# A graph layer on one core: the first layer norm folded into centred weights, with its row factors sent through DRAM

## The reference, cut to what matters

```
def _layernorm(x, axis=-1, eps=1e-05):
    m = jnp.mean(x, axis=axis, keepdims=True)
    v = jnp.var(x, axis=axis, keepdims=True)
    return (x - m) / jnp.sqrt(v + eps)

# graph layer: N_USER = N_ITEM = 10000, HID = 128
h = item_feat @ W_item.T + b_item
b = user_feat @ W_user.T + b_user
gnn = jax.nn.relu(adj @ h + b)

# an LSTM over the 10000 rows, then gated running sums of its states
x = x + gnn(_layernorm(x), ...)           # adj is 10000 x 10000, float32
x = x + ffn(_layernorm(x)[None], ...)[0]
```

## Time and profile before

| | us |
|---|---|
| median of 3 runs (1485.9 to 1490.18) | 1486.9 |
| the profiled execution | 1486.99 |
| its span, first to last instruction | 1485.2 |

### The profile page before, as it was taken

One profiled execution on the slowest core, in us unless ns is written; L12 is line 12 of the kernel. 1 busy time (PEld: TensorE's weight loads), 2 busy tenths in 40 slices (PEclk: granted clock), 3 DMA queues, 4 the chain that ended last, 5 costly groups with the idle time before them and its releaser, 6 DMA issues.

```text
span 1485.2 us, 25012 instructions
## 1 busy us (share of the span) xinstructions
PE 1449.2 (98%) x7584; PEld 1227.4 (83%) x7584; DVE 1218.3 (82%) x2027; ACT 1088.3 (73%) x1601; POOL 212.8 (14%) x189
## 2 busy tenths in 40 slices
PE   8999999999999999999999999999999799999994
PEld 7878888788778888888888888877888699999994
DVE  7998888888888888888888888888888566677677
ACT  5778777778777778777777787777778476556662
POOL 0000010000001001001001000000100032017775
PEclk9999999999999999999999999999999899999997
DMA  9889999999999999999999999999999203000003
GB/s 382 309 325 359 376 345 360 367 350 365 358 352 361 370 351 363 371 356 358 367 352 371 352 359 376 340 369 355 350 363 380 97 1 123 15 2 0 0 0 139
DMA packets 70515, 426.67 MB, mean 287 GB/s; under 512 B 8723, under 2 KB 17620, under 8 KB 70358
## 3 DMA queue, kind: packets, MB, share of 16 engines
q1 hardware_dynamic: 68896, 425.12, 76.6%
q10 hardware_dynamic: 1590, 1.18, 0.2%
HBM read 416.02 MB, written 10.24 MB: 287 GB/s over the span
## 4 chain that ended last, share of the span: by engine, by line
issue 79%; PE 19%; DVE 1%; POOL 0%; ACT 0%; POOLq 0%; DVEq 0%
PE psZ L848 10%; PE psZ L836 3%; PE psZ L837 2%; PE psZ L838 2%; PE psZ L854 1%; DVE u L1241 1%; PE psZ L824 0%; PE psZ L914 0%; POOL rstd L419 0%; POOLq L422 0%; ACT normed L557 0%; PE psZ L918 0%; DVE dif L1256 0%; PE psV L734 0%; DVE dif L1254 0%
## 5 line engine op out<-in xcount | busy, mean ns | idle before, releaser
L998 DVE TENSOR_TENSOR a_lo<-raw,a_hi 128x1000 fp32r<-128x1000 f32 (+1 forms) x800 | 917.3, 1182 | 108.4 <-ACT a_hi L586 101.9
L586 ACT ACTIVATE a_hi<-raw 128x1000 fp32r<-128x1000 f32 (+1 forms) x800 | 806.2, 1030 | 253.7 <-PE psG L759 170.6
L757 PE MATMUL psG<-a_hi,item_hi 128*128 128x500 f32 (+1 forms) x1580 | 635.5, 402 | 2.5 <-DVE a_lo L998 1.6
L759 PE MATMUL psG<-a_hi,item_lo 128*128 128x500 f32 (+1 forms) x1580 | 615.6, 390 | 0.0
L758 PE MATMUL psG<-a_lo,item_hi 128*128 128x500 f32 (+1 forms) x1580 | 612.2, 387 | 0.0
L757 PEld LDWEIGHTS psG<-a_hi,item_hi 128*128 128x128 f32 (+1 forms) x1580 | 296.4, 188 | 81.1 <-DVE a_lo L998 16.7
L759 PEld LDWEIGHTS psG<-a_hi,item_lo 128*128 128x128 f32 (+1 forms) x1580 | 297.7, 188 | 61.1
L758 PEld LDWEIGHTS psG<-a_lo,item_hi 128*128 128x128 f32 (+1 forms) x1580 | 297.3, 188 | 60.7 <-issue 4.4
L419 POOL TENSOR_TENSOR rstd<-var,minus_half 125x4 f32<-125x4 f32 x40 | 76.2, 1905 | 1096.8 <-DVE var L982 1096.8
L848 PE MATMUL psZ<-hist,wh 128*128 (+1 forms) x1264 | 169.8, 277 | 0.1
L848 PEld LDWEIGHTS psZ<-hist,wh 128*128 128x128 f32 x1264 | 154.0, 191 | 2.1 <-issue 0.6
(11 more groups left out here) (143 smaller groups left out, 809.4 us busy)
## 6 DMA issues: line engine op xcount, KB each, us to landing
raw<-in_adj_main SPq DMA_DIRECT2D x360, 1000.0 KB, 6.9
raw<-in_adj_main SPq DMA_DIRECT2D x40, 750.0 KB, 4.2
x_copy<-xb SPq DMA_DIRECT2D x20, 250.0 KB, 5.5
u<-x_copy SPq DMA_DIRECT2D x1, 5000.0 KB, 14.8
out<-u SPq DMA_DIRECT2D x25, 200.0 KB, 2.4
xb<-in_xT SPq DMA_DIRECT2D x18, 250.0 KB, 5.3
u<-in_itemT SPq DMA_DIRECT2D x8, 512.0 KB, 11.7
u<-in_itemT SPq DMA_DIRECT2D x1, 648.0 KB, 12.5
```

Of the source, the lines that this page charges most:

```text
L586: nc.scalar.activation(a_hi[:, s % CUT, 0:n], raw[:, r % RAW, at:at + n], ACT.Copy)\
L757: pe.matmul(bank, w_hi, hi, start=(c == 0), stop=False)
L759: last = pe.matmul(bank, w_lo, hi, start=False, stop=(c == CH))
L998: dve.tensor_tensor(a_lo[:, s % CUT, 0:n], raw[:, r % RAW, at:at + n], a_hi[:, s % CUT, 0:n].bitcast(f32), ALU.subtract).then_inc(lo_ready, 1)
```

## The change

Five edits go together.

1. **The first layer norm.** Subtracting the mean is moved into the user weights: `wu` is multiplied once by the centring matrix (PE at r = 3 of block 0, a DVE copy back). The scale is applied to x columns: the 500 factors `rstd1`, which lie as 125 partitions x 4, are stored to a row in DRAM by a DMA that ACT issues (`send_rstd`, r = 16), loaded back into all 128 partitions of `v` by a second ACT DMA (`spread_rstd`, r = 18), and DVE multiplies `v` by x (`scale_user`, r = 1 of the next block). The transposition back, `normalise` and `out_v` of the first norm go, and so does its `row_scale`. The product with `wu` moves from r = 2 to r = 3. Block 0 does the same at r = 2, 4, 6 and 8.
2. **Half-piece loads.** SP loads each half of a piece on its own semaphore, as soon as that half's slot is free; ACT waits for its half alone.
3. **The stacked chunk.** The tail of 16 rows is loaded three times, to partitions 0, 32 and 64; the weights beside them hold hi, hi and lo, and DVE turns the middle copy of `a_hi` into the remainder. PE then does one product over 80 rows instead of three over 16.
4. The store of the new x moves from r = 9 to r = 7.
5. In the LSTM, PE does four of the twelve input products of a step between the two groups' state products instead of three (`BETWEEN`).

The diff, cut to its core:

```diff
-AT = dict(relu=1, x1=2, bias=2, rows2=3, stats2=4, pair2=5, eps2=5, scale2=6, norm2=7, back2=8, out2=10,
-          rows1=12, stats1=13, pair1=14, eps1=14, scale1=15, norm1=16, back1=17, out1=19,
-          store=9, load=11, wx=10)
-FIRST = dict(rows=0, stats=1, scale=2, norm=3, back=4, out=5, bias=7)
+AT = dict(relu=1, x1=2, scaled=1, bias=3, rows2=3, stats2=4, pair2=5, eps2=5, scale2=6, norm2=7, back2=8, out2=10,
+          rows1=12, stats1=13, pair1=14, eps1=14, send=16, spread=18, store=7, load=11, wx=10)
+FIRST = dict(rows=0, stats=1, send=2, centre=3, centred=4, spread=4, scaled=6, bias=8)
...
+STACK = (0, 32, 64)
+STACKED = STACK[-1] + TAIL
+PASSES = [(q, part) for q in range(4) for part in range(3)]
+BETWEEN = 4
...
             def load_block(j, wait=True, move=True, prefetch=True, items={}):
                 for r in range(PIECES):
-                    if wait or r >= RAW:
-                        sp.wait_ge(lo_ready, HALVES * j + 2 * (r - RAW + 1))
-                    sp.dma_start(raw[:, r % RAW, 0:SIZES[r] * BW],
-                                 adj_main[j, :, STARTS[r] * BW:(STARTS[r] + SIZES[r]) * BW])\
-                        .then_inc(raw_in[r % RAW], 16)
-                    if r == LAST:
-                        sp.dma_start(raw[0:TAIL, r % RAW, SIZES[r] * BW:(SIZES[r] + 1) * BW], adj_tail[j])\
-                            .then_inc(raw_in[r % RAW], 16)
+                    for h in range(2):
+                        landed = raw_in[2 * (r % RAW) + h]
+                        n, at = half_cols(r, h)
+                        n -= BW * (r == LAST and h == 1)
+                        if wait or r >= RAW:
+                            sp.wait_ge(lo_ready, HALVES * j + 2 * (r - RAW) + h + 1)
+                        sp.dma_start(raw[:, r % RAW, at:at + n],
+                                     adj_main[j, :, STARTS[r] * BW + at:STARTS[r] * BW + at + n]).then_inc(landed, 16)
+                        if r == LAST and h == 1:
+                            for p0 in STACK:
+                                sp.dma_start(raw[p0:p0 + TAIL, r % RAW, at + n:at + n + BW], adj_tail[j])\
+                                    .then_inc(landed, 16)
...
-            def out_v(m):
-                act.wait_ge(ln_back, m + 1)
-                nc.scalar.activation(v[:, :], psV[:, 0:BW], ACT.Copy).then_inc(v_ready, 1)
+            def send_rstd(m):
+                act.wait_ge(ln_rstd, m + 1)
+                act.dma_start(rstd_dram[0:1, :].rearrange("o (s p) -> p (o s)", p=SW), rstd1[:, :],
+                              allow_slow_non_contiguous=True).then_inc(rstd_stored, 16)
+
+            def spread_rstd(j):
+                act.wait_ge(rstd_stored, 16 * (j + 1))
+                act.dma_start(v[:, :], rstd_dram[0:1, :].to_broadcast([P, BW])).then_inc(rstd_spread, 16)
...
-                    if has1 and r == AT["norm1"]:
-                        normalise(2 * j + 1)
-                    if has1 and r == AT["out1"]:
-                        out_v(2 * j + 1)
+                    if has1 and r == AT["send"]:
+                        send_rstd(2 * j + 1)
+                    if has1 and r == AT["spread"]:
+                        spread_rstd(j + 1)
...
+            def scale_user(j):
+                dve.wait_ge(rstd_spread, 16 * (j + 1))
+                dve.tensor_tensor(v[:, :], v[:, :], xb[:, j % 2, :], ALU.mult).then_inc(v_ready, 1)
...
+                            if c == CH:
+                                last = pe.matmul(bank, item_hi[0:STACKED, c * HID:(c + 1) * HID],
+                                                 a_hi[0:STACKED, s % CUT, i * BW:(i + 1) * BW], start=False, stop=True)
+                                continue
```

More of the change, by code:

```diff
@@ L134, in program @@
         bi_row = sb("bi_row", [1, HID], f32, first)
+        item_tail = sb("item_tail", [P, STACKED], f32, first)
         item_lo = sb("item_lo", [P, (CH + 1) * HID], f32r, first)
@@ L152, in program @@
         rstd = sb("rstd", [SW, SUB], f32, first)
+        rstd1 = sb("rstd1", [SW, SUB], f32, first)
         shift_rows = sb("shift_rows", [SW, SUB], f32, first)
@@ L200, in program @@
         wi_in = sem("wi_in")
+        item_tail_ready = sem("item_tail_ready")
         bi_in = sem("bi_in")
@@ L208, in program @@
         item_in = [sem(f"item_in{i}") for i in range(len(PARTS) - 1)]
-        raw_in = [sem(f"raw_in{s}") for s in range(RAW)]
+        raw_in = [sem(f"raw_in{s}") for s in range(2 * RAW)]
         xb_in = sem("xb_in")
@@ L415, in _, with inv_std @@
                     .then_inc(const_ready, 1)
-            def inv_std(m):
+            def inv_std(m, t):
                 pool.wait_ge(ln_eps, m + 1)
-                pool.tensor_tensor(rstd[:, :], var[:, :], minus_half[0:SW, :].to_broadcast([SW, SUB]),
+                pool.tensor_tensor(t[:, :], var[:, :], minus_half[0:SW, :].to_broadcast([SW, SUB]),
                                    ALU.pow).then_inc(ln_rstd, 1)
-            with nc.gpsimd.Fori(0, 2 * NB) as m:
-                inv_std(m)
+            inv_std(0, rstd1)
+            pool.memset(item_tail[:, :], 0.0).then_inc(item_tail_ready, 1)
+            pool.wait_ge(item_tail_ready, 1)
+            pool.wait_ge(item_in[-1], 16)
+            for at in STACK:
+                pool.tensor_copy(item_tail[:, at:at + TAIL], u[:, L + CH * P:L + N]).then_inc(item_tail_ready, 1)
+            inv_std(1, rstd1)
+            with nc.gpsimd.Fori(1, NB - 1) as j:
+                inv_std(2 * j, rstd)
+                inv_std(2 * j + 1, rstd1)
+            inv_std(2 * NB - 2, rstd)
+            inv_std(2 * NB - 1, rstd)
             pool.wait_ge(u_ready, NB)
@@ L721, in _, with to_rows @@
         def _(pe):
-            def to_rows(m, par):
-                if not (isinstance(m, int) and m == 0):
-                    pe.wait_ge(ln_normed, m)
+            def to_rows(par, reader=None, count=0):
+                if reader is not None:
+                    pe.wait_ge(reader, count)
                 for s in range(SUB):
@@ L727, in to_rows, with to_columns @@
                 last.then_inc(ln_rows, 1)
[L729 to L732, removed]
+            def to_columns(count):
+                pe.wait_ge(ln_normed, count)
                 for s in range(SUB):
@@ L762, in body @@
                         pe.wait_ge(x_in[0], 16)
-                        to_rows(0, 0)
-                    if items and r == FIRST["back"]:
-                        to_columns(0)
+                        to_rows(0)
+                    if items and r == FIRST["centre"]:
+                        pe.wait_ge(wu_in, 32)
+                        pe.matmul(psW[:, 0:HID], centre[:, :], wu[:, :], start=True, stop=True).then_inc(wu_psum, 1)
                     if items and r == AT["wx"]:
@@ L797, in item_quad @@
                     pe.wait_ge(item_sum, q - 1)
+                if q == QUADS - 1:
+                    pe.wait_ge(item_tail_ready, 1 + len(STACK))
                 for c in range(4 * q, min(4 * q + 4, CH + 1)):
-                    rows = P if c < CH else TAIL
-                    last = pe.matmul(psI[0:rows, q % 2, (c % 4) * HID:(c % 4 + 1) * HID],
-                                     u[:, L + c * P:L + c * P + rows], wi[:, :], start=True, stop=True)
+                    rows = P if c < CH else STACKED
+                    columns = u[:, L + c * P:L + (c + 1) * P] if c < CH else item_tail[:, :]
+                    last = pe.matmul(psI[0:rows, q % 2, (c % 4) * HID:(c % 4 + 1) * HID], columns, wi[:, :],
+                                     start=True, stop=True)
                 last.then_inc(item_psum, 1)
@@ L828, in from_input_f32, with from_input @@
                         last.then_inc((z0_ready, z1_ready)[bank][0], 1)
-            def from_input(gates, row, par, late=0):
-                for q in gates:
+            def from_input(passes, row, par, late=0):
+                for q, part in passes:
                     w_hi, w_lo = (w[:, q * HID:(q + 1) * HID] for w in (wx_hi, wx_lo))
@@ L997, in split_lo @@
                 dve.wait_ge(hi_ready, HALVES * j + s + 1)
-                dve.tensor_tensor(a_lo[:, s % CUT, 0:n], raw[:, r % RAW, at:at + n],
-                                  a_hi[:, s % CUT, 0:n].bitcast(f32), ALU.subtract).then_inc(lo_ready, 1)
+                tail = s == HALVES - 1
+                m = n - BW if tail else n
+                last = dve.tensor_tensor(a_lo[:, s % CUT, 0:m], raw[:, r % RAW, at:at + m],
+                                         a_hi[:, s % CUT, 0:m].bitcast(f32), ALU.subtract)
+                if tail:
+                    mid = slice(STACK[1], STACK[1] + TAIL)
+                    last = dve.tensor_tensor(a_hi[mid, s % CUT, m:n], raw[mid, r % RAW, at + m:at + n],
+                                             a_hi[mid, s % CUT, m:n].bitcast(f32), ALU.subtract)
+                last.then_inc(lo_ready, 1)
             def item_sum_part(q):
@@ L1041, in body @@
                         eps(0)
-                    if items and r == FIRST["scale"]:
```

(8 more changed lines are left out.)

109 lines of the change are left out of this document (59 added, 50 removed).

## The result

The changed kernel took 1560.4 us (median of 4 runs, 1558.0 to 1562.9) beside 1488.0 of the kernel before: a ratio of 1.049, 95% interval 1.046 to 1.051. The forecast was 1533 us, in a range of 1462 to 1585. Its profiled execution took 1562.94 us, its span 1561.1, 75.9 longer than before.

The account below looks back on a forecast made before the run. PE was taken to bound ordinary blocks, loads running close behind. From 1487.0 us: -8.8 transpositions, -1.5 slow step, -9.0 tail, -3 late loads, +68 waits for the factors' store, giving 1533 us; range 1462 to 1585.

Parts of the forecast that it names:

- The late store: ACT's wait after r = 18: store lands 10.0 us after issue, PE loses 3.6 us a block, +68; chance 0.47.
- the likeliest case: The late store taken alone: 1533 us in all, between 1495 and 1575; chance 0.47.
- The clock: Rival: each wait in stage one also halves PE's clock, up to 2.5 us more a block, 1580 us; chance 0.08.
- counted once: Block 0's two waits at a slower pace, entered as one of nineteen waits of 3.6 us.
- The price by five engines: Store of 125 partitions on 5 engines, 100 runs each: 23.5 us to landing were it not for the stream's running dry.
- The gains: All savings with the store in time: 22.3 us, giving 1464.7 us; that rival's chance 0.34.
- The tail: PE's end of block: one product of 80 rows instead of three, 0.45 us saved 20 times, -9.0 us.
- The late loads: Stage one's adjacency loads: half-pieces save between nothing and 5.2 us, taken as -3.
- The transpositions back: PE, first norm: 20 groups of four go, 0.44 us each, -8.8 us.
- The slow step of 0.085: PE behind the product with `wu`: one slow step goes in 18 blocks, -1.5 us.
- What follows stage one: The LSTM: order of PE's input passes worth nothing, 1 us allowed either way.
- The loads as the bound: Rival: stage one's blocks limited by loads at 362 GB/s, 57.6 us each, 1498 us in all; chance 0.04.

Follow-up runs that it names:

- e1_no_wait: Changed kernel with every DMA kept, but ACT's wait for the factors' store after r = 18 removed in ordinary blocks: 1557.5 us, ratio 1.048 to the kernel before.
- e9_apart64: Changed kernel with load-back steps moved behind the store's landing, ordinary blocks' 500 single factors stored 64 bytes apart in a spare tensor: 1455.7 us, ratio 0.978.
- e2_block0: Changed kernel with only block 0's steps moved later (spread r 4 to 9, scaled 6 to 12, bias 8 to 14): 1533.5 us, ratio 1.032.
- e10_runs16: Changed kernel, steps unmoved, factors stored as 125 runs of 16 bytes, PE's first-norm transpositions taking every fourth column: 1463.3 us, ratio 0.984.
- e12_permuted: Changed kernel, steps unmoved, factors stored as 125 runs of 16 bytes, VectorE restoring the order by reading v with stride four: 1458.0 us, ratio 0.981.
- e4_old_norm: Changed kernel with the first norm as in the kernel before; half-piece loads, stacked chunk, store at r = 7 and BETWEEN = 4 kept: 1464.9 us, ratio 0.986.
- e8_scattered: Changed kernel with load-back steps moved behind the store's landing, ordinary blocks' 500 single factors stored 4 KB apart in a spare tensor: 1454.8 us, ratio 0.978.

## Where the prediction was right, and where not

*The late store* was the likeliest case, and slower is what came. Its landing was put at 10.0 us; 8.9 to 11.2 were measured. Added idle time of 3.6 us a block was forecast; (68.1 - 3.1)/18 = 3.6 came. That both numbers agree is luck, for the reason given is not the cause. The prediction had the store's runs take turns with the adjacency's, so that ACT alone is late. In ordinary blocks the 500 runs start together, 2.2 to 2.9 us after the issue in the block at 508.04 (the trace's DMA records), and it is the adjacency that is held up: from 6 to 10 us after that issue its runs of 4000 bytes take 1.2 to 1.7 us each in the mean, where 0.16 is usual. With the wait gone (e1_no_wait) the same time is lost on late pieces, and with the elements apart (e9_apart64) nothing is lost. The step that failed is that all of it is put down to the wait, with the loads beside it costing nothing.

*The clock* had a chance of 0.08 as a case of its own, with up to 2.5 us a block. It came with the late store: 22.6 us in 18 blocks, 1.3 each. That is what the forecast lacked in the ordinary blocks: it has them 45 us slower (3.6 times 18, less nine tenths of 22.3), and they were 63.3 slower: 65.0 of idle gaps and 22.0 at half clock, less 23.7. The stops lie inside dense work, which the prediction held against a fall; behind 13 of the 18 stops after a store the granted clock fell to 0.50 all the same.

*Block 0* was "counted once", 3.6 us. It cost 15.0; e2_block0 gives 12.7 of it back. There the store took 19.4 us while the loads flowed (361 GB/s in its last 6 us), and its 500 runs start spread over some 15 us: there they do take turns, and there the wait was the loss. With 125 runs (e10_runs16) the store in the same place took 7.9 us; on five engines these are 75 runs each fewer, 0.15 us a run. The price by five engines that the prediction gave in its sentence on the Trainium skill, 23.5 us, is nearer here than my 10.0. Why runs take turns in block 0 and not later was not tried.

*The gains* were put at 22.3 us. With a harmless store they are 28.4 (e12_permuted) to 32.5 (e9_apart64). The tail was mis-sized: the one product of 80 rows has neither the slow entry nor the long first step that I kept. In e4_old_norm it starts at 537.23, and the next product at 537.46:

```profile
537.00 0.39 PE L777 MATMUL psG<-a_hi,item_lo 128*128 128x500 f32 x1
537.23 0.39 PE L768 MATMUL psG<-a_hi,item_hi 80*128 80x500 f32 x1
537.46 0.39 PE L775 MATMUL psG<-a_hi,item_hi 128*128 128x500 f32 x1
```

In the kernel before, the rows behind those of the earlier trace rows show that the products after the tail were slow too:

```profile
545.26 0.49 PE L757 MATMUL psG<-a_hi,item_hi 128*128 128x500 f32 x1
545.59 0.39 PE L758 MATMUL psG<-a_lo,item_hi 128*128 128x500 f32 x1
```

That is two steps (0.45) and four long entries (0.38) less: 0.83 a block, not 0.45. A block without late loads fell by 1.09 in e4_old_norm, from 56.69 to 55.60; the other 0.26 lies in PE's ordinary steps, 0.2256 instead of 0.2267 us in the mean, and its cause was not tried. The late loads of the earlier trace rows went almost whole, 5.0 of 5.2 us, not 3. But the stop at the end of block 0, which those windows leave out, grew from 1.6 to 2.8 us, with products at half clock behind it, and that interval lost 3.0 us more than before: 2.0 are left. The transpositions back gave 55.60 - 55.18 = 0.42 a block, where 0.44 was forecast. The slow step of 0.085 gave nothing: in e12_permuted the product with `wu` stands directly before the transpositions, and the block takes the same 55.18 as in e9_apart64, where it stands apart. What follows stage one fell by 2.3 us, in e4_old_norm too (2.0), where 1 either way was allowed; which edit did it was not tried. The upper end of the likeliest case is 1574 by its own terms, not 1575.

*The loads as the bound* fell: e8_scattered moves more bytes than the kernel before, in blocks of 55.2 where 57.6 were to be the bound. VectorE never waited for the load into `v`, as forecast.

## What to carry to other kernels

Here a DMA of single elements to neighbouring addresses cost what it did to the other transfers, more than its own latency: look at the GB/s beside the busy share, since engines that are 0.95 busy at 53 GB/s are stuck. Hiding the wait for it was worth nothing in the ordinary blocks (12.7 us in block 0); making each run longer (16 bytes), and putting the order right on an engine with slack, took the whole loss away. Take the suspected wait out before rebuilding around it.

## What the runs showed of the hardware that I had not expected

500 writes of 4 bytes into one row of 2000 bytes held all transfers down to 45 to 83 GB/s from 3 to 9 us after the issue (19 stores of the changed kernel), where 500 writes 64 bytes apart left 248 to 301. The Trainium skill ("DMA: Bandwidth & Descriptors", Specifications) says that a transfer below 512 bytes is a read-modify-write. That alone does not tell the two apart; that the distance between the writes decides is what the runs add. The same page of the Trainium skill ("Latency and other measured facts", on back-pressure in transfers between cores) says that stalled writes also stall the other queues of their DMA engine. Loads on SP's queue standing still behind ACT's store would fit that, but here all is on one core, and no run separates the engine from the memory.

Whether PE's clock falls after a stop does not follow from the stop's length alone. In the changed kernel, the stop of 4.2 us at 576.7 was followed by 12 products at half clock and the one of 2.4 us at 517.3 by none; but 2.5 us at 218.5 had nine, and 3.2 us at 759.2 had none.
